# Wide products of a fused conditional kernel: three passes into the left bank, then three into the right, instead of left and right by turns

## The reference, cut to what matters

```
x = x + _L0_cond_ref(x, lengths, ...)                                   # convolution
x = x + jnp.einsum('bct,bcd->bdt', x, weights[condition])               # channel mix
x = x + jnp.einsum('bsd,od->bso', x, base_weight) + base_bias + lora_2  # dense
x = x + jnp.einsum('bsi,oi->bso', x, W) + lora_3 * 0.5                  # dense
```

## Time and profile before

| | |
|---|---|
| median of 3 runs | 1430.96 us |
| the profiled execution's own time | 1429.82 us |
| its span (first to last instruction) | 1427.9 us |
| TensorE (PE) busy | 1421.3 us, 100% of the span |
| weight loads (PEld) busy | 1317.4 us, 92% |
| VectorE (DVE) busy | 1125.3 us, 79% |
| ScalarE (ACT) busy | 612.3 us, 43% |
| GpSimd (POOL) busy | 100.9 us, 7% |

### The profile page before, as it was taken

One profiled execution on the slowest core, in us unless ns is written; L12 is line 12 of the kernel. 1 busy time (PEld: TensorE's weight loads), 2 busy tenths in 40 slices (PEclk: granted clock), 3 DMA queues, 4 the chain that ended last, 5 costly groups with the idle time before them and its releaser, 6 DMA issues.

```text
span 1427.9 us, 31106 instructions
## 1 busy us (share of the span) xinstructions
PE 1421.3 (100%) x9274; PEld 1317.4 (92%) x9274; DVE 1125.3 (79%) x2256; ACT 612.3 (43%) x1217; POOL 100.9 (7%) x187
## 2 busy tenths in 40 slices
PE   9999999999999999999999999999999999999999
PEld 8888899999999999999999999999999999999998
DVE  7975498888888887787887787788788788778875
ACT  4331276666666664433443333343343344333332
POOL 2322100000000001010000000000000000000000
PEclk9999999999999999999999999999999999999999
DMA  8032188888888878565565566456556556555552
GB/s 318 1 143 67 60 287 275 273 272 274 274 273 274 275 264 228 175 192 152 172 190 167 156 191 187 156 178 194 155 180 188 152 170 192 169 156 191 187 156 82
DMA packets 117091, 272.98 MB, mean 191 GB/s; under 512 B 23928, under 2 KB 60155, under 8 KB 114399
## 3 DMA queue, kind: packets, MB, share of 16 engines
q1 hardware_dynamic: 107126, 238.91, 54.4%
q10 hardware_dynamic: 9934, 33.68, 5.8%
HBM read 199.60 MB, written 72.88 MB: 191 GB/s over the span
## 4 chain that ended last, share of the span: by engine, by line
PE 97%; SPq 1%; DMA 1%; DVE 1%; issue 0%; POOL 0%; POOLq 0%; DVEq 0%
PE ps L822 18%; PE ps L815 17%; PE ps L1745 14%; PE ps L814 12%; PE ps L793 8%; PE ps L1628 7%; PE ps L1756 6%; PE ps L831 4%; PE ps L1736 3%; PE ps L1614 2%; PE ps L1748 2%; PE ps L1648 1%; PE ps L1637 1%; PE ps L1674 1%; PE ps L409 0%
## 5 line engine op out<-in xcount | busy, mean ns | idle before, releaser
L815 PE MATMUL ps<-weights,xa 128*128 128x352 f32 x1152 | 321.2, 322 | 0.0
L814 PE MATMUL ps<-weights,xa 128*128 128x256 f32 x1152 | 318.8, 279 | 0.1
L822 PE MATMUL ps<-weights,xs 128*128 128x512 f32 x1152 | 292.4, 402 | 0.0
L822 PEld LDWEIGHTS ps<-weights,xs 128*128 128x128 f32 x1152 | 207.1, 189 | 41.6
L572 ACT ACTIVATE a<-ps 128x512 f32<-128x512 f32 x128 | 76.8, 600 | 362.8 <-PE ps L793 362.8
L1745 PE MATMUL ps<-toep,ut 128*128 128x512 f32 (+2 forms) x1152 | 226.7, 342 | 0.0
L814 PEld LDWEIGHTS ps<-weights,xa 128*128 128x128 f32 x1152 | 216.9, 188 | 4.3 <-issue 3.4
L815 PEld LDWEIGHTS ps<-weights,xa 128*128 128x128 f32 x1152 | 216.0, 187 | 0.5
L1745 PEld LDWEIGHTS ps<-toep,ut 128*128 128x128 f32 x1152 | 194.3, 189 | 16.6
L793 PEld LDWEIGHTS ps<-m_gath,x_in 128*128 128x128 f32 x1024 | 131.0, 191 | 6.8 <-DVE x_in L670 1.5
L793 PE MATMUL ps<-m_gath,x_in 128*128 128x128 f32 x1024 | 135.0, 275 | 1.1 <-DVE x_in L670 1.1
(11 more groups left out here) (233 smaller groups left out, 2250.7 us busy)
## 6 DMA issues: line engine op xcount, KB each, us to landing
xt<-in_xt SPq DMA_DIRECT2D x64, 512.0 KB, 5.7
x_d<-yo SPq DMA_DIRECT2D x64, 512.0 KB, 2.9
x_nat<-in_x SPq DMA_DIRECT2D x64, 512.0 KB, 4.2
lags<-kern_d SPq DMA_DIRECT2D x63, 512.0 KB, 4.9
x_in<-x_d SPq DMA_DIRECT2D x62, 512.0 KB
out<-y_out ACTq DMA_DIRECT2D x62, 512.0 KB, 4.5
stack<-b_d SPq DMA_DIRECT2D x130, 128.0 KB, 4.2
tab<-a_d SPq DMA_DIRECT2D x128, 128.0 KB, 2.1
```

Of the source, the lines that this page charges most:

```text
L814: mm(acc[:, left, 0:HALF], x_part, w[:, 0:HALF], start=start, stop=end, skip_group_check=True)
L815: ins = mm(acc[:, right, 0:HALF + KR], x_part, w[:, HALF:WIDE], start=start, stop=end, skip_group_check=True)
L822: ins = mm(acc[:, bank], operand[:, a, i, :], plain(i, b, m), start=opens and i == a == b == 0, stop=i == K4 - 1 and a == 1, skip_group_ch ...
```

## The change

For each chunk the two banks are now served one after the other: all three passes into the left bank, then all three into the right. Before, each pass served left and right by turns. Both versions issue the same 24 matmuls and 24 weight loads for a product, with the same operands and the same widths. In each bank the sums are taken in the same order. Line 814 now stands for both matmuls.

```diff
             for i in chunks:
-                for a, b in PASSES:
-                    start, end = opens and i == a == b == 0, i == K4 - 1 and a == 1
-                    x_part, w = operand[:, a, i, :], wide(i, b, m)
-                    mm(acc[:, left, 0:HALF], x_part, w[:, 0:HALF], start=start, stop=end, skip_group_check=True)
-                    ins = mm(acc[:, right, 0:HALF + KR], x_part, w[:, HALF:WIDE], start=start, stop=end, skip_group_check=True)
+                for bank, first, end_col in ((left, 0, HALF), (right, HALF, WIDE)):
+                    for a, b in PASSES:
+                        start, end = opens and i == a == b == 0, i == K4 - 1 and a == 1
+                        ins = mm(acc[:, bank, 0:end_col - first], operand[:, a, i, :], wide(i, b, m)[:, first:end_col],
+                                 start=start, stop=end, skip_group_check=True)
             return ins
```

## The result

In 6 runs of each on one chip, the changed kernel takes 1436.34 us (1435.55 to 1440.28) and the kernel before 1430.78 us (1430.59 to 1431.38). By the two medians that is +5.6 us, or 0.39%, where the forecast was 1434.3 us (+3.3). The ratio on record, which is not that of the two medians, is 1.0047, with a 95% interval from 1.0036 to 1.0057.

A forecast was written before the change was run, and what follows sets the result against it. TensorE's start-to-start distances were taken as the bound. 256 chunks at 12 ns plus 256 at 2 ns gave 3.6 us, less 0.3 for pairs already high: +3.3, forecast 1434.3 us (slower by 0.23%), range 1429.0 to 1438.5.

The forecast's parts named there:

- The bound: TensorE, busy 1421.3 of 1427.9 us, has no idle time; only its start-to-start distances can change the time.
- Banks: In the wide products, three matmuls in a row accumulating into one bank cost 0.
- The stationary block: In a chunk, two loads instead of four fetch the block already there; this costs 0.
- Width: Short matmuls behind short ones lose their cheap place between long ones; a chunk goes to 832 ns from 820 or 830.
- the left triple: Three 256-column matmuls in a row take 352 ns, 117.3 each, against 342 before at the lowest level.
- the right triple: Three 352-column matmuls in a row take 480 ns, bounds 477 and 484, against some 477 to 483 before.
- The low base: Before the change, a chunk was taken as 820 ns in M1 and M5 and 830 in M2 and M4.
- a rival with a chance of 0.12: Full surcharge of steady runs on every matmul in the wide products: 840 ns a chunk, 1438.2 us; chance 0.12.
- the forecast case: Wide products at 832 ns a chunk, +3.3 us, 1434.3 us; own range 1432.5 to 1436.5, chance 0.46.
- The reason given: In a couple, the short matmul is limited by the load beside it, some 7 ns over streaming; the long by streaming, 12.5 over.
- The rival "no change": The surcharge of wide-product matmuls doesn't depend on the neighbours' width; 1431.0 us, chance 0.28.
- The rival "faster": Every wide product falls to the lowest level, 819 ns a chunk, 1427.9 us; chance 0.14.

The follow-up runs named there:

- e1_skew: Against the kernel before: banks and widths still by turns, passes shifted so blocks load in the changed kernel's sequence; 1430.38 us against 1429.70, ratio 1.0008.
- e7_perm: Against the kernel before: weight blocks of M1 and M2, and of M5 and M4, exchanged in memory; 1432.16 us against 1430.70, ratio 1.0008.
- e12_shift: Against the kernel before: every buffer in SBUF moved 128 bytes further on; 1430.57 us against 1430.91, ratio 0.9996.
- e3_304: Against the kernel before: still by turns, but the 608 columns cut 304 and 304, not 256 and 352; 1432.84 us against 1429.70, ratio 1.0020.

## Why the prediction was right in sign, and where it fell short

**The bound.** Right. TensorE has no idle time, and 6.8 us more of start-to-start distance in the wide products became 6.3 us of span. The waits fell by 0.7 us, so none of the cost is a wait.

**Banks: 0.** Right, and now shown for these widths and not only for 512 columns: with the bank changing at every matmul and the widths in threes, the cost stays (842 ns a chunk).

**The stationary block: 0.** Right (e1_skew, 828 ns with the new sequence of loads).

**Width: the term of the sum.** The mechanism was right in that, of the three respects, only the order of the two slices counts: 13 ns a chunk at 256/352, nothing in the mean at 304/304. The size was off, in both terms. I took 352 ns for the left triple, from the low-rank and the convolution rows; over all 512 it was 356. I took 480 ns for the right triple, from the surcharge of steady runs; it was 486, above the 484 that I had set as its upper end. Together a chunk took 842, not 832. The low base was half of the matter: M1 and M5 went from 820 to exactly 840 ns, thus to the full surcharge of the steady runs, which I had kept for a rival with a chance of 0.12. M2 and M4 went from 830 to 843, where the forecast had 832. The rival's 840 ns was nearer in the trace than my forecast. Its time, 1438.2 us, is 1.9 us above the median measured, mine 2.0 below; in the trace its sum is the better one, since it is made against 825 ns as the mean of before, and that mean was 829.

Two errors offset each other in my +3.3: a chunk after was 10 ns dearer than summed (+5.1 us), and a chunk before was 4 ns dearer than taken (-1.9 us, of which I had allowed for 0.3). That the measured 1436.34 us lies inside the forecast case's own range, which ends at 1436.5, is partly luck.

**The reason given** was that the short matmul is held by its load and the long one by its streaming. That is not shown. The sums of M1 and M5 are near it at every cut: with 114 ns for the short one and streaming and 12.5 ns for the long one a couple would take 280 ns at 240/368 (measured 280) and 286.5 at 224/384 (measured 289), and it gives no gain at 288/320 (measured 280, the full surcharge). Against it stand four things. First, at 224/384 the recorded starts put the cost on the long matmul. Second, M2 and M4 take 277 ns a couple at 304/304 and 288/320, where it gives 280. Third, some pairs pay 3.36 us in M5 by turns at 256/352. Fourth, it doesn't say why a short matmul behind a short one takes 120 ns, since that one has its load beside it as well. What makes 256/352 by turns cheap stays open. In most pairs it goes with the streamed block (e7_perm), it doesn't go with the absolute place (e12_shift), of the cuts tried it needs this one, and runs of three already destroy it. Where the right slice starts in its block, and how it lies to the loaded block, were not tried by themselves.

**The rival "no change"** fell: the runs of 512 columns, equal in both orders, say nothing on unequal widths, as the forecast had noted. The rival "faster" fell too; no product reached 3.28 us in the new order.

For an isolated matmul the Trainium skill (TensorE: Matmul & The Clock Gate, section Back-to-back issue gap) gives N/2.4 + 2.5 ns, and it says that in a stream of loads and matmuls both set the spacing. An estimate by that formula is 775 ns for a chunk in any order. The traces of this stream have 828 to 867 for the same 1824 streamed columns, so the formula doesn't describe it.

## What to carry to other kernels

Where TensorE is the bound, count start-to-start distances over a whole period and not durations. The order of matmuls of unequal width is worth some ns each: here 13 ns for every six, 0.4% to 0.5% of the kernel. Don't take the price of one arrangement from another that looks like it: threes in the convolution were near the steady rate, by turns there gained nothing, and yet the same swap cost the wide products 13 ns a chunk. Try the few orders and cuts, since they are cheap to write. Of the cuts by turns here, 224/384 was much the dearest (1.3%), and 240/368, 288/320 and 304/304 lay within 0.2% to 0.25% of 256/352.

## What the runs showed of the hardware that I had not expected

- With the operands of fp32r and a load for each matmul, the distance per matmul is streaming plus 13.3 ns in several steady arrangements: 120 ns at 256 columns (rows 8), 140 at 304 in M1 and M5 of e3_304, 226.7 at 512 (rows 10), and 280 ns for 256 and 352 in M5 after the change. It isn't a constant: 304 columns take 138.4 ns in M2 and M4 of e3_304.
- The same product can stand on several levels (3.28, 3.32, 3.36, 3.40 us) from pair to pair with the same instructions, and the level changes where one product gives way to the next.
- At 224/384 a matmul starts 0.10 us behind its own load's start, and the short one's distance reads 0.10 us, the long one's 0.19, with a sum of 289 ns.
- Exchanging weight blocks in memory moves the low level of 3.28 us from M5 (29 of 32 pairs, then 1) to M4 (3, then 23); moving everything in SBUF by 128 bytes leaves it in M5 (28 of 32).
